# Identity transposes in front of the causal stage's products with the values

## The reference

```python
x = x + attn_a(layernorm(x))      # 8 heads of 64, rank 64 keys and values
x = x + ffn(layernorm(x))         # 2 layers: local attention (window 128), gated MLP
x = x + attn_b(layernorm(x))      # 16 heads of 16, causal
x = x + ffn(layernorm(x))

def attn_b(x):                    # what the change touches
    q, k, v = split(x @ w_qkv + b_qkv)                 # per head
    dot = q @ k.T
    vals = sum(q * q) + sum(k * k).T
    scores = dot * dot / (vals - 2.0 * dot + 1e-6)
    scores = scores + causal_mask
    return (softmax(scores) @ v) @ w_out + b_out
```

## Time and profile before

| | |
|---|---|
| time, median of 3 runs | 4387.95 us (4383.82 to 4391.58) |
| profiled execution, its own time | 4387.66 us |
| its span | 4385.6 us |
| mean granted clock of TensorE | 0.954 of full |
| TensorE busy | 4091.2 us (93%) |
| VectorE busy | 3252.5 us (74%) |
| ScalarE busy | 2536.5 us (58%) |
| GpSimd busy | 1732.1 us (39%) |

### The profile page before, as it was taken

The page is one execution under the profiler, slowest core; times in us unless marked ns, Lnnn a source line. Parts: engine busy times, 40 slices in busy tenths (PEclk is TensorE's granted clock), DMA queues, the critical chain, the costliest instruction groups (busy, mean ns, idle before and its releaser), DMA issues.

```text
span 4385.6 us, 65645 instructions
## 1 busy us (share of the span) xinstructions
PE 4091.2 (93%) x23120; PEld 2606.4 (59%) x23120; DVE 3252.5 (74%) x7689; ACT 2536.5 (58%) x5481; POOL 1732.1 (39%) x1816
## 2 busy tenths in 40 slices
PE   8999999999999999987888888888999999999997
PEld 4666556666666666554555555555666666666664
DVE  6667677777667667669999999988677676677663
ACT  5556554454444454449888899876544544444441
POOL 2223365555556556420000001013555565465541
PEclk9999999999999999988888888888999999999999
DMA  2000000000010000000000000101000000100000
GB/s 80 11 16 6 25 11 6 3 3 6 23 30 15 8 8 10 24 22 18 23 20 23 23 26 19 36 18 35 3 6 3 3 25 8 35 15 18 13 20 22
DMA packets 63174, 78.60 MB, mean 18 GB/s; under 512 B 15312, under 2 KB 47488, under 8 KB 62848
## 3 DMA queue, kind: packets, MB, share of 16 engines
q1 hardware_dynamic: 62848, 74.40, 5.9%
HBM read 36.65 MB, written 12.58 MB: 11 GB/s over the span
## 4 chain that ended last, share of the span: by engine, by line
PE 69%; DVE 14%; issue 8%; ACT 7%; POOL 1%; DMA 0%; SPq 0%; DVEq 0%; ACTq 0%; POOLq 0%
PE wide L873 47%; PE o_ps L873 9%; PE wide L876 7%; PE turn_ps L876 5%; ACT prob L1238 2%; DVE w_up L1396 2%; DVE w_up L1402 2%; PE turn_ps L873 1%; DVE prob L1414 1%; DVE x L1408 1%; DVE turned L1339 1%; DVE turned L1353 1%; DVE ss L1346 1%; DVE hid L1408 1%; ACT turned L1166 1%
## 5 line engine op out<-in xcount | busy, mean ns | idle before, releaser
L873 PE MATMUL wide<-x,w_up 128*128 128x512 f32 (+3 forms) x2528 | 844.7, 550 | 4.4 <-DVE x L1505 2.4
L873 PE MATMUL wide<-w_in,x_t 128*128 128x512 f32 (+2 forms) x1920 | 811.0, 566 | 2.6 <-ACT x_t L1156 1.3
L1618 POOL TENSOR_SCALAR prob<-prob,st 128x256 f32<-128x256 f32 (+1 forms) x1024 | 552.5, 559 | 578.5 <-DVE st L1438 576.5
L1238 ACT ACTIVATE prob<-prob,st 128x256 f32<-128x256 f32 (+1 forms) x1024 | 479.7, 470 | 166.4 <-DVE st L1425 166.0
L873 PE MATMUL o_ps<-pt,v 128*32 128x128 f32 (+2 forms) x5120 | 512.1, 346 | 57.5 <-DVE pt L1458 31.5
L873 PEld LDWEIGHTS wide<-x,w_up 128*128 128x128 f32 (+2 forms) x2528 | 379.4, 198 | 296.3 <-issue 279.0
L873 PEld LDWEIGHTS wide<-w_in,x_t 128*128 128x128 f32 x1920 | 344.1, 193 | 337.9 <-issue 330.6
L1599 POOL TENSOR_TENSOR rn<-ss,minus_half 128x16 f32<-128x16 f32 x128 | 434.9, 3397 | 138.8 <-DVE ss L1348 135.2
L1591 POOL TENSOR_TENSOR sines<-raw,rot 128x512 f32<-128x512 f32 x256 | 355.0, 1408 | 341.0 <-ACT raw L1163 341.0
L873 PEld LDWEIGHTS o_ps<-pt,v 128*64 128x64 f32 (+1 forms) x5120 | 324.1, 133 | 268.8 <-issue 131.3
L1425 DVE CUSTOM_DVE_ANT_0 prob<-wide,local_mask 128x256 f32<-128x256 f32 (+1 forms) x1024 | 334.4, 382 | 137.5 <-PE wide L873 137.5
(11 more groups left out here) (161 smaller groups left out, 7392.3 us busy)
## 6 DMA issues: line engine op xcount, KB each, us to landing
kept<-resid SPq DMA_DIRECT2D x16, 512.0 KB, 2.6
x<-kept SPq DMA_DIRECT2D x16, 512.0 KB, 3.3
w_up<-hid SPq DMA_DIRECT2D x62, 128.0 KB, 2.2
x<-hid SPq DMA_DIRECT2D x62, 128.0 KB, 2.3
shifted<-resid SPq DMA_DIRECT2D x32, 224.0 KB
w_in<-in_f_wqkv SPq DMA_DIRECT2D x4, 1536.0 KB, 6.5
w_up<-in_f_w SPq DMA_DIRECT2D x4, 1492.0 KB, 7.2
resid<-in_x SPq DMA_DIRECT2D x8, 512.0 KB, 7.9
```

The costliest lines, as they stand in the source:

```text
L873: return eng.matmul(out, lhsT, rhs, start=start, stop=stop, skip_group_check=True)
L1238: last = eng.activation(pr[:, local_span(t)], pr[:, local_span(t)], ACT.Exp, bias=sm[:, t:t + 1], scale=-1.0, accum_out=sm[:, 4 + t:5 + t])
L1618: last = eng.tensor_scalar(pr[:, local_span(t)], pr[:, local_span(t)], sm[:, 8 + t:9 + t], 1.0, ALU.mult, ALU.mult)
```

## The change

The planner also returns the start and the end that it gave each part. When TensorE's program comes to a mix of the causal stage, it looks at the part that went into turn_ps last. If the planner has all of that part's readers done by the start of this mix, TensorE waits for those readers' semaphore and then turns the identity three times, by transposes of 128 columns, into three quarters of turn_ps. Nothing reads the result. Otherwise nothing is put in.

```diff
+SPARE = 3
...
-        end[part] = stop + LANDING.get(kind, 0.0)
+        start_of[part], end[part] = start, stop + LANDING.get(kind, 0.0)
...
-    return order, place, before, queues
+    return order, place, before, queues, start_of, end
...
-ORDER, PLACE, HELD, QUEUES = ordered()
+ORDER, PLACE, HELD, QUEUES, START, END = ordered()
...
             pe.wait_ge(S["ident"], 16)
+            narrow = None
+
+            def keep_busy(part):
+
+                if narrow and all(END[r] <= START[part] for r in readers_of(narrow) if r in END):
+                    psum_read(pe, narrow)
+                    for c in range(SPARE):
+                        tr(turn_ps[:, c * P:(c + 1) * P], ident[:, :])
+
             for part in ORDER["PE"]:
                 kind, u, i = part
                 s, n, b = u % 2, u // SEQS, u % SEQS
                 ps = buffers.get(PLACE.get(part))
+                if PLACE.get(part) == f"bank{BANKS - 1}":
+                    narrow = part
+                if kind == "mix" and stage_of(u) == "b":
+                    keep_busy(part)
                 for held in HELD.get(part, ()):
                     psum_read(pe, held)
```

More of the change, by code:

```diff
@@ L491, in ordered @@
     order = {e: [] for e in free_at}
-    end, place, before = {}, {}, {}
+    start_of, end, place, before = {}, {}, {}, {}
     holders = [None] * BANKS
```

## The result

The changed kernel takes 4397.02 us (median of 12 runs, 4388.7 to 4403.32) against 4388.6 (12 runs, 4383.82 to 4396.99). The ratio of the two is 1.0019, with a 95% interval of 1.001 to 1.0028: 4 to 12 us slower. The forecast was 4392 in a range of 4372 to 4407, with 0.34 for slower by over 0.2% and 0.44 for within it; the measured 0.19% lies right at that border.

What follows compares the result with a forecast made beforehand. VectorE was taken to bound the causal stage. Sets on its path cost 7 us and the returning clock gives back 3, so +4 on the profiled 4387.66 us makes 4392 us, range 4372 to 4407.

Steps and rivals of the forecast that it cites:

- The bound: Causal stage, 1960 to 2960 us: VectorE sets the pace, busy 947 of 1000 us, with ScalarE close behind at 881.
- The prediction's sign for this, 2 us: Stages outside the causal one: the forecast is wrong if they change by more than 2 us.
- The added wait: TensorE's wait before a set for the copy out of turn_ps: costed at nothing, at most 0.6 us each if uncovered.
- The size of a set: Three transposes on TensorE: 0.35 us at full clock, 0.63 at half, 0.44 on average; 51 us for 115 sets.
- Which sets reach the end: Of 115 sets in the causal stage, 95 miss idle time and 17 lie on VectorE's path, costing 7 us.
- Rival 2: Causal stage: ScalarE passes the delay on, so 45 sets cost 20 us, less 3 from the clock: +17, 4405 us; chance 0.20.
- What the clock gives back: Causal stage: a quarter of 307.6 us at half clock returns, 77 us, worth 2.7 us to VectorE.
- At 3.5 points of VectorE's time: Causal stage: VectorE idles 7.7% at half clock and 4.2% outside it; this prices the 77 returned us at 2.7 us.
- The upper bound that I gave, 23.7 us: Most the returning clock could save in the causal stage: the time VectorE idles in the half-clock stretches.
- Transposes and the clock: TensorE's transposes count as work like any other for the full clock, read from one rise with six sevenths transposes behind it.
- Rival 3: Causal stage: transposes do not hold the clock up, so 7.5 us are paid and nothing returns: 4395 us; chance 0.09.
- Rival 1: Causal stage: the clock comes back nearly whole, saving VectorE about 17 us for 6 of sets: -11, 4377 us; chance 0.21.

Runs made afterwards that it cites:

- the wait alone: Changed kernel with the added wait kept at its 115 places but no transposes after it: 4388.18 us, ratio 0.9995 to the kernel before.
- the pairs: Changed kernel's transposes replaced by plain products using 4 or 128 rows: 4451.94 against 4401.42 us (three of 96 columns), 4454.84 against 4418.13 (two of 64).
- The runs with 4 and 128 rows: Changed kernel with each set's three transposes replaced by three products of 96 columns: 4451.94 us with 4 rows, 4401.42 with 128.
- the shorter pair: Changed kernel with each set's three transposes replaced by two products of 64 columns: 4454.84 us with 4 rows, 4418.13 with 128.
- the planned gaps: Against the changed kernel, identity transposes only where the planner has TensorE idle, at most 8 each (95 places, 379 transposes): 4371.89 us, ratio 0.9957.

## Why the prediction came out right, and where it did not

**The bound.** Right. VectorE sets the pace, and nothing outside the stage moved: before 1960 us and behind 2960 us VectorE's and TensorE's busy times are within 5 us of before. The prediction's sign for this, 2 us, was finer than one trace can tell: the span grew by 4.9 us and the stage by 7.8, and the stage's first product with the values starts anywhere from 1942 to 1949 us in these kernels.

**The added wait, at nothing.** Right: the wait alone is at 0.9995.

**The size of a set.** Too low. It was the slope of a long row, 0.35 us; in place it is 0.48, and 0.78 instead of 0.63 at the half clock: 62 us in all for the 51 that I had. A slope leaves out the first instruction of a group.

**Which sets reach the end, 7 us.** This step failed. It counted only sets in front of VectorE's own waits (17 of 115), as if a set between two waits were absorbed. Rival 2 had ScalarE's waits count too, 20 us, and they did grow: 50 to 62 us at the products behind the sets. What a set costs is not measured by itself, but it can be estimated. By all executions 48 us of half clock came back. The executions of the kernel before differ among themselves, and their time goes with their half clock at 0.24 us for each (71 executions, correlation 0.71, which need not all be cause); the pairs say 0.31 to 0.43, with longer sets in place. So what came back is worth some 11 to 21 us, and for the sum of 8 the sets must have cost 19 to 29 of their 62 us, where the prediction had 7. That is an estimate; no run shows the two terms apart.

**What the clock gives back.** The amount was near in the traces: I let 77 us return and put the half clock near 230 us; it is 253 between 1960 and 2960 us, the mean clock 0.87 as forecast. By all executions it is 48, since the trace that I started from had more half clock than most. The price was wrong. "At 3.5 points of VectorE's time" compared how much VectorE idles on average while the clock is half and while it is full. The runs with 4 and 128 rows put ten times as much on each microsecond. Most of the time so lost lies inside the half-clock stretches: of the 47 us that VectorE idles more with 4 rows than with 128, 41 are there (83.6 us of 403.0 against 42.6 of 262.8), and of the 40 us of the shorter pair 39. So the loss is not hidden elsewhere; the average share of idle time before the change (7.7%) did not tell what it becomes with sets in TensorE's queue (11.8% with the change, 16% and 21% with the longer ones). Why it rises so steeply no run takes apart. The upper bound that I gave, 23.7 us, is what VectorE idles at the half clock in one trace; no kernel here gained more than the 14 to 24 us of the planned gaps. In this change both errors had opposite signs and the same order, so the sum of +4 came out near the measured +8. That is luck: the mechanism as I had it (two small terms, 7 and 3) is not what the pairs and the averages say.

**Transposes and the clock.** As predicted, and against the rule of the Trainium skill ("TensorE: Matmul & The Clock Gate", Part 4) that the full clock does not engage for them: in the traces three transposes a set took 72 us off the half clock and six took 137 (48 and 124 by all executions). Sets of two plain products of all 128 rows, 0.08 us longer, took off none (369 us against 345; 402 against 385). Rival 3 is out. That transposes alone bring the full clock is not shown, as they run here among products.

**Rival 1.** Its cause, a clock that comes back nearly whole, did not come at these places, where 273 us stayed. Where the sets fill planned idle time 201 us stayed, and the kernel gained 14 to 24 us, more than the 11 that rival 1 gave. So its sign and size were in reach at other places, but nowhere did the clock come back nearly whole.

**What stays open.** What a set costs apart from its clock, beyond the estimate above; why VectorE loses so much more in a half-clock stretch when sets are in it; whether 4-row products harm by anything but the clock; and why sets in front of the score products did less than those in front of the turned weights, which I did not follow up.

## What to carry to other kernels

Price the half clock by an experiment with work that holds it up and equal work that does not, not by the average share of time that the pacing engine idles while it is half. Take the clock from many executions, since the half clock of one kernel went from 341 to 423 us. Work put in to keep the clock up belongs where the schedule is known to be idle, sized to that gap; with about as many transposes (345 and 379), the place and the size of the sets made the difference between 0.2% slower and 0.4% faster. When two terms of unknown price work against each other, a small sum says nothing about either.

## What the hardware showed beyond that

Products with 4 rows of weights and data in place of 128, at the same places and about the same length, left 403 us instead of 263 at the half clock in the traces, and 449 instead of 300 in the whole program by all executions. And more time on TensorE did not mean less half clock: three transposes of 128 columns (0.48 us) left 273 us, two products of 64 columns and 128 rows (0.56 us) left 369, three of 96 columns (0.81 us) 263; by all executions 337, 402 and 300.

The same kernel does not get the same clock each time. Of the 71 executions of the kernel before, the 16 with a mean clock of 0.954 or less took 4395 us on average, the 13 with 0.959 or more 4383.
